# A gated cross-attention layer with routed experts: VectorE's sums move between two steps of the head scaling

## The reference

```python
kv   = concat([layernorm(ctx) @ Wkv.T, layernorm(x) @ Wlkv.T])   # 64 + 1024 keys
q    = layernorm(x) @ Wq.T                                       # 4 heads of 64
attn = softmax(mask(rmsnorm(q) * SCALE @ rmsnorm(k).T))
x    = x + tanh(g_xattn) * ((attn @ v) @ Wo.T + bo)
y    = layernorm(x)
probs = softmax(y @ w_router)                                    # 8 experts, the top 2 are used
x    = x + tanh(g_ffn) * sum over the 2 of weight * (gelu(y @ w1[e] + b1[e]) @ w2[e] + b2[e])
```

## Time and profile before

| | us |
|---|---|
| three runs | 906.76, 902.59, 905.99; median 905.99 |
| profiled execution, its own time | 906.47 |
| its span, first to last instruction | 904.7 |
| mean granted TensorE clock | 0.987 |
| start of the first scores (window 0, group 0) | 39.79 |
| start of the last group's scores (window 7, group 8) | 457.40 |

### The profile page before, as it was taken

The page is one execution under the profiler, slowest core; times in us unless marked ns, Lnnn a source line. Parts: engine busy times, 40 slices in busy tenths (PEclk is TensorE's granted clock), DMA queues, the critical chain, the costliest instruction groups (busy, mean ns, idle before and its releaser), DMA issues.

```text
span 904.7 us, 19559 instructions
## 1 busy us (share of the span) xinstructions
PE 855.7 (95%) x5968; PEld 657.3 (73%) x5968; DVE 645.3 (71%) x1500; ACT 511.5 (57%) x1371; POOL 289.5 (32%) x241
## 2 busy tenths in 40 slices
PE   3898999999999999999999999899999999999995
PEld 3654555545555455555469999899999999999995
DVE  6766777768777667676897777775755776676695
ACT  2668875787857877468841843443433443353462
POOL 2321212221265212641054238332332322232233
PEclk8899999999999999999999999999999999999998
DMA  4801000130012201120044649352442535362272
GB/s 128 248 1 50 1 1 1 47 96 1 7 54 82 94 1 56 50 94 1 2 137 99 181 82 259 58 144 47 96 90 43 137 72 114 47 145 45 37 230 27
DMA packets 71896, 70.26 MB, mean 78 GB/s; under 512 B 18593, under 2 KB 66977, under 8 KB 71841
## 3 DMA queue, kind: packets, MB, share of 16 engines
q1 hardware_dynamic: 57696, 52.73, 20.0%
q0 software_dynamic: 13152, 16.86, 10.9%
q10 hardware_dynamic: 992, 0.00, 0.1%
HBM read 44.04 MB, written 26.31 MB: 78 GB/s over the span
## 4 chain that ended last, share of the span: by engine, by line
PE 56%; DVE 17%; issue 13%; POOL 8%; ACT 4%; DMA 1%; another core or an unknown queue 0%; SPq 0%; POOLq 0%; DVEq 0%; ACTq 0%
PE psS L1705 22%; PE psF L1901 10%; PE psO L1901 10%; DVE p_sum L1141 6%; PE psS L1822 4%; POOL rr L681 4%; POOL routed L691 3%; PE psO L1838 3%; PE psF L1705 2%; PE psF L1869 1%; ACT sq L828 1%; DMA xr<-in_x 1%; PE psO L1850 1%; DVE Q L1124 1%; PE psO L1705 1%
## 5 line engine op out<-in xcount | busy, mean ns | idle before, releaser
L889 ACT ACTIVATE V<-psS,b_col 128x256 f32<-128x256 f32 x280 | 116.9, 470 | 214.8 <-PE psS L1705 195.3
L699 POOL DMA_INDIRECT out<-V,token_i x70 | 121.5, 1736 | 261.8 <-DVE V L1332 240.5
L872 ACT ACTIVATE p_ring<-psS,shift 128x1024 f32<-128x1024 f32 x128 | 136.6, 1111 | 71.7 <-PE psS L1822 69.7
L681 POOL TENSOR_TENSOR rr<-ssm,minus_half 128x4 f32<-128x4 f32 (+1 forms) x72 | 76.1, 1057 | 282.4 <-DVE ssm L1105 282.4
L1838 PE MATMUL psO<-p_ring,V 128*64 128x512 f32 x576 | 148.5, 612 | 0.0
L1141 DVE TENSOR_TENSOR p_sum<-p_sum,p_ring 128x1024 f32<-128x1024 f32 (+1 forms) x112 | 135.7, 1211 | 1.3
L1901 PE MATMUL psF<-ln_hi,K 128*128 128x256 f32 x560 | 124.2, 285 | 0.2
L1822 PEld LDWEIGHTS psS<-Q,K 64*128 64x128 f32 x864 | 77.0, 187 | 61.3 <-issue 41.9
L1822 PE MATMUL psS<-Q,K 64*128 64x512 f32 x864 | 121.3, 413 | 0.0
L1901 PE MATMUL psO<-ln_hi,K 128*128 128x256 f32 x560 | 120.5, 279 | 0.0
L1309 DVE CAST K<-V 128x512 fp32r<-128x512 f32 x140 | 60.4, 431 | 59.1 <-ACT V L889 57.0
(11 more groups left out here) (297 smaller groups left out, 1766.5 us busy)
## 6 DMA issues: line engine op xcount, KB each, us to landing
xr<-in_L_ffn_w SPq DMA_DIRECT2D x11, 1024.0 KB, 8.2
xn<-in_L_ffn_w SPq DMA_DIRECT2D x11, 1024.0 KB, 5.6
lnf<-routed SPq DMA_DIRECT2D x35, 258.0 KB
routed<-pad_rows SPq DMA_DIRECT2D x17, 258.0 KB, 9.9
xr<-in_x SPq DMA_DIRECT2D x8, 512.0 KB, 4.5
xb<-in_x SPq DMA_DIRECT2D x4, 1024.0 KB, 6.1
out<-xb SPq DMA_DIRECT2D x4, 1024.0 KB
b_raw<-in_L_ffn_b SPq DMA_DIRECT2D x11, 128.0 KB, 3.5
```

Of the source, the lines that this page charges most:

```text
L681: pool.tensor_tensor(rr[0:p, c % 2, n], ssm[0:p, c % 2, n], minus_half[0:p, n], ALU.pow).then_inc(rr_ready, 1)
L699: pool.indirect_dma_start(out_rows, bass.IndirectOffsetOnAxis(ap=token_i[:, m:m + 1], axis=0), y_out[:, m, :], None, bounds_check=NTOK - 1 ...
L872: act.activation(p_ring[0:p, u % RING, :], psS[u % 2][0:p].rearrange("p a n -> p (a n)"), ACT.Exp, bias=bias).then_inc(exp_done, 1)
L889: act.activation(g32[:, q % 2, (c % 2) * TM:(c % 2 + 1) * TM], psH[q][:, (c % 2) * TM:(c % 2 + 1) * TM], ACT.Gelu_apprx_tanh, bias=b1_col[ ...
```

## The change

Three things move. In the groups that project a tile, other than groups 0 and 5 of a window and group 3 of windows 3 and 5 (`routed_here`), the addition of unit 2g-2 goes behind `mean_squares`, ahead of `scale_heads`. `norm_offsets` of sequence 1 goes from group 5 of window 0 to group 4, behind the same group's other steps. `plan_experts` goes behind `turned_lo(8)` and `take_meta(8)` of tile 7. TensorE's tile 5 is written out, and its loop opens with tile 6. Nothing is added to or taken from the arithmetic.

```diff
--- before.py
+++ after.py
@@ -1465,7 +1465,10 @@
                     waited = past and i < 2 if even else more and i in (1, 3)
                     if waited:
                         heads_lo(turned_at(g))
-                    if g >= 1:
+                    summed = summed_at(g) is not None
+                    routed_here = not even and past and not last and i == 3
+                    between = tile_at(g) is not None and g >= 1 and i != 0 and i != 5 and not routed_here
+                    if g >= 1 and not between:
                         add_probabilities(2 * g - 2)
                     if not even and past and last and i == 2:
                         router_logits(b - 1)
@@ -1480,9 +1483,10 @@
                         heads_lo(turned_at(g))
                     if tile_at(g) is not None:
                         mean_squares(tile_at(g))
-                    if not even and past and not last and i == 3:
+                    if between:
+                        add_probabilities(2 * g - 2)
+                    if routed_here:
                         router_logits(b - 1)
-                    summed = summed_at(g) is not None
                     if g >= 1 and not ahead and summed:
                         add_probabilities(2 * g - 1)
                     if not even and past and not last and i == 6:
@@ -1496,7 +1500,7 @@
                         norm_lo(b + 1, i)
                     if even and past and i == 5:
                         second_offsets(b - 1)
-                    if even and more and b == 0 and i == 5:
+                    if even and more and b == 0 and i == 4:
                         norm_offsets(b + 1)
                     if i == 1 and w >= 1:
                         denominators(2 * w - 1)
@@ -1630,8 +1634,6 @@
                 for t in range(5, KTILES):
                     for q in range(NQ):
                         activate(t, q)
-                    if t == 7:
-                        plan_experts()
                     move_meta(t)
                     turned_lo(t + 1)
                     take_meta(t + 1)
@@ -1646,6 +1648,7 @@
                         if t == 6:
                             plan_ends()
                         if t == 7:
+                            plan_experts()
                             plan_switches()
                         results(t)
                         if t == 6:
@@ -1986,7 +1989,12 @@
                 second_layer(4)
                 ranks(B - 1)
 
-                with pe.Fori(5, SURE - 1) as t:
+                for t in range(5, 6):
+                    first_layer(t)
+                    turn_tile(t + 1)
+                    second_layer(t)
+
+                with pe.Fori(6, SURE - 1) as t:
                     first_layer(t)
                     turn_tile(t + 1)
                     second_layer(t)
```

## The result

The changed kernel takes 911.43 us, the median of four runs (908.65 to 912.16), against 904.84 us (902.59 to 906.76) of the kernel before beside it. The ratio is 1.0072, with a 95% interval of 1.0052 to 1.0093: slower by 6.6 us. The forecast was 912.0 us, 6.0 above the median known then.

The account below looks back on a forecast made before the run. TensorE was taken to bound the kernel. The profiled 906.5 us, +7.6 in the attention and -1.6 for the plan gave 912.5, as a median 912.0 us; own range 909 to 915, 8 in 10 within 900 to 918.

Parts of the forecast that it names:

- The power under an addition: Moved groups of the attention: GpSimd's power hardly advances under VectorE's addition, so clamp to scaling takes 2.20 us, not 1.29.
- The rule beside it: Two-input VectorE and GpSimd SBUF operations exclude each other, first starter wins; each shift would be 1.05 us, not 0.91.
- The moved additions: Forty groups, windows 0 to 6: scaling 0.91 us later where ScalarE sets the clamp, 0.33 earlier where VectorE is late.
- The largest term, +4.6: Group 5 of windows 2 to 6: all of the 0.91 us lands on TensorE's wait for the sums, five times.
- The offsets: Window 0: ScalarE's 1.92 us wait for the offsets goes, TensorE still waits 0.8 us for the power; -0.8 us.
- The plan: Experts, tile 7: TensorE's 1.56 us wait for the low part of tile 8's rows goes, -1.6 us; 0 if hidden.
- The loop: Experts: writing out TensorE's tile 5 changes no matmul and costs 0, with bounds of -5.4 and +5.4 us.
- rival 3: The stall around tile 7 goes with the loop's new start (906.6 us, chance 0.14) or grows (917.4 us, 0.06).
- The 5.4 us that the forecast called unexplained: Experts: what tiles 7 and 8 (31.2 us) took beyond two calm ones (24.3 us), less the plan's 1.56 us.
- rival 1: Moved groups: the power is not slowed, TensorE's waits in the attention shrink by 8.6 us, 896 us in all; chance 0.10.
- Rival 2: Attention: the delay is hidden more often, only the five group-5 waits stay (+4.6 us), 906.7 us in all; chance 0.12.
- Rival 4: The order of instructions on the chip is not the one written; chance 0.01.

Follow-up runs that it names:

- spacer: The changed kernel with a 128x256 reduction (0.41 us) between clamp and moved addition: 899.25 us; the same with additions moved in only 14 groups: 894.24 us.
- the offsets' kernel: The kernel before with only the offsets of sequence 1 computed one group earlier: 901.32 us, ratio 0.9968.

## Why the prediction was right

**The power under an addition.** Right. The forecast read 2.20 us from clamp to scaling off group 0; it is 2.21. The reading that the pair of instructions makes it, and not what else runs in group 0, is borne out by the reduction in the addition's place (1.01 us) and by the 72 powers after, whose median is the six slow ones' length. The forecast also wrote that the addition always comes first. It did in 39 of the 40 groups. In the one at 309.97 us VectorE stood for 0.28 us without a releaser, the addition began 0.20 us after the power, and the power took 1.01 us.

**The rule beside it.** Each shift was costed at 0.91 us by the row, and group 5 of windows 2 to 6 shows 0.91 to 0.93. The price by the Trainium skill (SBUF — State Buffer, section "SBUF: two separate sides"), with the power taking its full time after the addition, was an estimate of 1.05 us for each step. The trace doesn't agree on that size: the power ends 0.86 us after the addition in this group. That the one that starts first excludes the other is borne out when the addition is first, in every case. It isn't when the power is: the additions behind it took at most 1.22 us in all 54 groups with a spacer, and in 3 of them it was the power, the first to start, that was held up.

**The moved additions.** Every term of the sum is within 0.25 us of its measured size, and what was said to be hidden is hidden: in the other moved groups nothing changes by more than 0.05 us. What the forecast rests on is that each group was carried through by its own spare time, with 0.14 us in the barest one. The largest term, +4.6, was foreseen as a wait that is already late by 0.16 us and takes over all of the 0.91.

**The offsets.** The term was -0.8 and came to -0.56; the turn waits 0.71 us where 0.8 was written. Alone the edit gives 1.62: the slower power takes back the rest.

**The plan.** The wait of 1.56 us is gone, as forecast. It is gone in all six profiles with the plan moved and there in three of the four without, so the edit removes it where it is; the forecast had said that another execution might not have it. The turns of tiles 7 and 9 are 28.0 to 31.2 us apart in those four (mean 29.4) and 26.7 to 28.5 in the six (mean 27.7), a difference of the forecast's size, from one execution each. In the profiled execution the whole part behind the last scores is 3.7 us shorter, and not 1.6. Of the rest, 0.93 us is the low granted clock in tile 8 of the kernel before, 0.87 went in tile 2 (which lasts 11.84 to 13.62 us over the ten profiles, and 13.27 with the plan alone moved) and 0.44 in tile 7 (the other parts took 0.1 back). Nothing shows any of it to be the plan's. In the medians 6.6 us less the attention's 7.7 is -1.1, with some 1.9 us to each side.

**The loop.** Cost at 0, measured at a ratio of 0.9999 (0.9983 to 1.0015). The stall around tile 7 neither went nor doubled (rival 3). It comes in the profiles of all ten kernels at the same tile, wherever the loop begins: TensorE's first stand without a releaser lies 10 to 13 us behind the turn of tile 7, and 7 us in the offsets' kernel. The 5.4 us that the forecast called unexplained hold the 0.93 us of the low clock; the stall itself was smaller. The forecast gave ScalarE's 10.22 us as a stall too. About half of that is ordinary waiting: the tile's first matmuls start at 558.26 and its first gelu at 564.78, 6.52 us behind, where in tile 8 it is 1.73 (577.54 and 579.27); some 4.8 us are the stall. Its cause was not settled. One lead was left untested: in the kernel before the DMA engines' busy share is 1.00 or more from 540 to 561 us, the longest such stretch, and the stands begin 3 us behind its end.

**The rivals.** The powers are slowed, so rival 1 fell as a forecast, but its number for the case without it, -8.6 us, was met by -8.42. Rival 2 fell on the groups 7, 3 and 4, which do cost. Rival 4 fell with the timeline.

## What to carry to other kernels

Idle time of an engine is not free for another instruction if what it waits for is then slowed by that instruction: read the waiting pair where the trace already has it, and take its step, not the single durations. Then ask of each place how much spare time stands between it and the engine that bounds the kernel; the same edit gained in the groups where VectorE was late and lost in those where it was not, and to apply it to the first alone, behind a short instruction that lets the power start first, made a loss of 0.7% into a gain of 1.0%, where the other three edits alone gained 0.27%. And look at all the instances of such a pair, not at one: the spacer failed in 3 of 54.

## What the runs showed of the hardware

- A GpSimd power of 128x4 took 1.01 us under a VectorE reduction with one SBUF input (1.22 us), and 1.92 us under an addition with two (1.23 us), both begun 0.17 us ahead of it. In all ten profiles every power that an addition was ahead of was held up, and ended 0.86 to 0.91 us after the addition did.
- With the addition begun 0.15 to 0.17 us after the power, 51 of 54 powers took 1.01 to 1.04 us and 3 took 2.24 to 2.25 us, again ending 0.87 us after the addition. The additions took 1.20 to 1.22 us in all of them.
- The granted clock at the start differs from execution to execution (a mean of 0.79 or 1.00 over the same 8 us), and goes with 1.8 us between the two profiled ones. In the experts a stretch at 0.50, behind four stands of TensorE of 0.3 to 0.5 us each, cost the kernel before 0.93 us.
- In all kernels TensorE stands for a few pieces of up to about 1 us around tiles 7 and 8 with no releaser, and ScalarE's gelus come late there, by some 4.8 us in the kernel before. It was not tried what removes it.
